# Forty unread products become fifty-four, and one gate-and-up product moves between two halves of a router's logits

## What is computed

```python
x = x + _L0_xattn_ref(_layernorm(x), ctx_2048)      # x, ctx to fp8 with scales, then one projection
x = x + _L0_ffn_ref(_layernorm(x), ...)             # 32 experts, 4 of them a token, one shared expert
x = x + _L1_xattn_ref(_layernorm(x), ctx_2048, ...) # 8 heads of softmax attention
x = x + _L1_ffn_ref(_layernorm(x), ...)             # 8 experts, 2 of them a token, shared expert
# _L0_ffn_ref:
logits = xf @ router_w.T + router_b
top_vals, top_idx = jax.lax.top_k(logits, K)
rw = softmax(top_vals) * SCALE
g, u = silu(x @ gate_w[e].T), x @ up_w[e].T
routed = sum over the chosen e of rw[e] * ((g * u) @ down_w[e].T)
shared = (silu(xf @ shared_gate_w.T) * (xf @ shared_up_w.T)) @ shared_down_w.T
```

## Time and profile before

| what | us |
|---|---|
| median of 3 runs | 417.14 (416.56 to 417.24) |
| the profiled execution | 417.1 |
| its span, first to last instruction | 415.3 |
| PE busy | 346.5 (83%) |
| DVE busy | 262.7 (63%) |
| ACT busy | 194.0 (47%) |
| POOL busy | 183.3 (44%) |

### The profile page before, as it was taken

The page is one execution under the profiler, slowest core; times in us unless marked ns, Lnnn a source line. Parts: engine busy times, 40 slices in busy tenths (PEclk is TensorE's granted clock), DMA queues, the critical chain, the costliest instruction groups (busy, mean ns, idle before and its releaser), DMA issues.

```text
span 415.3 us, 8257 instructions
## 1 busy us (share of the span) xinstructions
PE 346.5 (83%) x2383; PEld 195.8 (47%) x2383; DVE 262.7 (63%) x722; ACT 194.0 (47%) x453; POOL 183.3 (44%) x338
## 2 busy tenths in 40 slices
PE   0003298779999999999999978999987799998997
PEld 0002095444554555555454577666554354543455
DVE  2999848826555555555555488999877455555184
ACT  1341164344555555555554127999922445552110
POOL 2000300366766666676663107666610666753000
PEclk9999999999999999999999999999976999999899
DMA  7999993049222222323464387920011222331531
GB/s 227 396 255 333 319 266 106 1 139 281 88 97 88 93 90 89 103 85 95 113 186 158 125 333 215 255 59 2 2 47 56 85 82 88 100 95 39 175 106 51
DMA packets 28297, 57.32 MB, mean 138 GB/s; under 512 B 3806, under 2 KB 12734, under 8 KB 28254
## 3 DMA queue, kind: packets, MB, share of 16 engines
q1 hardware_dynamic: 20110, 37.85, 29.7%
q0 software_dynamic: 6528, 17.83, 14.1%
q10 hardware_dynamic: 1616, 1.11, 0.9%
HBM read 44.72 MB, written 12.06 MB: 137 GB/s over the span
## 4 chain that ended last, share of the span: by engine, by line
PE 69%; DVE 16%; issue 5%; ACT 4%; POOL 3%; DMA 2%; DVEq 0%; SPq 0%; ACTq 0%; POOLq 0%
PE bank L1308 22%; PE bank L1337 14%; PE bank L1319 6%; PE bank L1187 6%; PE bank L1299 4%; PE bank L1386 2%; PE bank L1398 2%; PE bank L1226 2%; PE bank L1200 2%; DMA x_sb<-x 2%; ACT arena L669 2%; DVE st L733 1%; DVE x_sb L1025 1%; PE bank L1154 1%; PE bank L1181 1%
## 5 line engine op out<-in xcount | busy, mean ns | idle before, releaser
L1308 PE MATMUL bank<-arena,xT 128*64 x272 | 111.2, 491 | 1.1 <-ACT xT L631 1.1
L1311 PE MATMUL bank<-xn,xT 128*64 128x384 f32 (+1 forms) x272 | 111.2, 491 | 0.0
L516 POOL DMA_INDIRECT xg<-m_xn,tab x68 | 66.2, 973 | 60.6 <-PE bank L1299 30.8
L505 POOL DMA_INDIRECT m_ys<-ysb,dest x68 | 67.2, 988 | 38.9 <-DVE ysb L945 22.4
L1337 PE MATMUL bank<-arena,hT 96*64 (+1 forms) x272 | 70.6, 381 | 2.4 <-DVE hT L931 2.3
L1340 PE MATMUL bank<-xn,hT 96*64 96x256 f32 (+1 forms) x272 | 70.7, 382 | 0.0
L624 ACT ACTIVATE xn<-arena 128x768 f32 (+1 forms) x68 | 56.3, 827 | 22.4 <-issue 22.4
L957 DVE TENSOR_TENSOR hh<-sg,bank 128x192 f32<-128x192 f32 (+1 forms) x71 | 24.8, 349 | 60.3 <-ACT sg L647 60.3
L1337 PEld LDWEIGHTS bank<-arena,hT 96*64 96x64 f32 (+1 forms) x272 | 34.7, 135 | 39.7 <-issue 29.3
L631 ACT ACTIVATE xT<-bank 128x256 f32<-128x256 f32 x71 | 27.2, 384 | 48.1 <-PE bank L1299 47.9
L925 DVE COPY xn<-arena 96x512 f32 (+1 forms) x68 | 29.2, 430 | 23.4 <-issue 23.4
(11 more groups left out here) (182 smaller groups left out, 564.9 us busy)
## 6 DMA issues: line engine op xcount, KB each, us to landing
arena<-w_gu SPq DMA_DIRECT2D x3, 3456.0 KB, 20.1
arena<-w_dn SPq DMA_DIRECT2D x3, 1728.0 KB, 26.5
arena<-m_ys SPq DMA_DIRECT2D x8, 512.0 KB, 6.5
arena<-w_gu SPq DMA_DIRECT2D x2, 1408.0 KB
m_xn<-xn SPq DMA_DIRECT2D x2, 1024.0 KB, 7.6
arena<-m_ys SPq DMA_DIRECT2D x8, 256.0 KB, 3.5
arena<-w_dn SPq DMA_DIRECT2D x2, 704.0 KB
arena<-w_gu SPq DMA_DIRECT2D x1, 1152.0 KB, 11.1
```

Of the source, the lines that this page charges most:

```text
L505: nc.gpsimd.indirect_dma_start(out=ys_d[L.name], out_offset=bass.IndirectOffsetOnAxis(ap=dest[:, s:s + 1], axis=0), in_=ysb[:, s % BUFS, : ...
L516: nc.gpsimd.indirect_dma_start(out=xg[:, b, :], out_offset=None, in_=xn_d[L.name], in_offset=bass.IndirectOffsetOnAxis(ap=d["tab"][:, s:s ...
L1308: T.matmul(bank[2 + s % 2][0:BLOCK, 0:2 * J2], xT[:, s % 2, c, 0:BLOCK], arena[:, bass.ds(off + c * 2 * J2, 2 * J2)], start=(c == 0), stop ...
L1311: return T.matmul(bank[2 + s % 2][BLOCK:P, 0:2 * J2], xT[:, s % 2, c, BLOCK:P], gu2[:, s % 2, cols], start=(c == 0), stop=(c == C - 1), ti ...
```

## The change

Three edits on PE's program. No other engine's program is changed.

```diff
+            def unread(n, b):
+
+                for _ in range(n):
+                    T.matmul(bank[b][:, 0:P], ident[:], ident[:], start=True, stop=True)
+
@@ routing
                 for i in range(NT // 2):
                     if L is L0 and i == 2:
+                        pe.wait_ge(*w_in)
+                        pe.wait_ge(x1_ready, NT)
+                        shared_steps(L, "early", 0, n_early[L.name], 0, 1)
                         turn_rows(L, 2)
                         turn_rows(L, 3)
@@
                 N = n_early[L.name]
                 pe.wait_ge(*w_in)
-                if L is L0:
-                    shared_steps(L, "early", 0, N, 0, 1)
-                else:
+                if L is L1:
                     pe.wait_ge(att_ready, NT)
@@
             pe.wait_ge(small_in, 64)
+            unread(14, 7)
             routing(L0, rw0, (w_shared, 32))
@@
-            def unread(n):
-
-                for _ in range(n):
-                    T.matmul(bank[5][:, 0:P], ident[:], ident[:], start=True, stop=True)
-
-            unread(26)
+            unread(26, 5)
             scores(0)
             scores(1)
             for p in range(nheads // 2):
                 turn_p(2 * p)
                 if p == 0:
-                    unread(14)
+                    unread(14, 5)
```

## The result

| kernel | median us | executions | ratio to before | 95% interval |
|---|---|---|---|---|
| before, in the same rounds | 418.76 | 16, 416.52 to 419.86 | | |
| changed | 415.47 | 16, 414.15 to 417.64 | 0.9932 | 0.9915 to 0.9949 |

The change is faster by 0.68% of 418.76, 2.85 us (2.1 to 3.6). The ratio is not that of the two medians: they differ by 3.29 us, the two means by 2.71. The three executions shown ahead of the prediction (417.14) were on the quick side of a kernel that scatters over 3 to 4 us, and the changed kernel's profiled execution (416.41 us, span 414.7) is on the slow side of its own. Set against the earlier trace rows, its trace shows the following.

What follows compares the result with a forecast made beforehand. PE at its slow clock was taken to bound the path through logits, mask and sums. Second-half logits 2.1 us earlier, 1.0 of late start included, less 0.1 for collision: 417.1 - 2.0 = 415.1 us, range 413.4 to 418.0.

Steps and rivals of the forecast that it cites:

- The path through logits and mask: Layer 0 routing: logits, mask and sums are one path on PE and DVE; all behind it, tiles included, starts 2.0 us earlier.
- Fourteen products raise the clock and it lasts: PE before the routing: the clock rises at 51.0 to 53.2 us, and both sets of sixteen logits take near 2.0.
- late start: First transposes on PE: products end at about 53.0 instead of 52.03, a cost of 1.0 us that nothing hides.
- The moved step: Between the logit halves: holds PE 1.3 us at the fast clock, now on the path; PE would have waited about 0.5.
- POOL beside DVE, 0.1: POOL's multiplication of the moved step falls beside DVE's second half; the collision costs the mask 0 to 0.5 us, taken as 0.1.
- The clock falls before step 1: PE is empty from 60.5 to about 64.1 us, so step 1 is expected slow again, as before.
- Rival B: Early shared steps: the clock rises one step later and step 2 pays 1.5 us, giving 416.6; chance 14%.
- The sum, 2.0: Whole kernel: second-half logits 2.1 us earlier, less 0.1 for the collision, carried through to the end.
- The time itself, 415.1: Whole kernel: profiled execution of 417.1 us less 2.0; likeliest case 414.5 to 415.7, at 54%.

Runs made afterwards that it cites:

- e9: The changed kernel run once more with nothing changed; 0.9937 of before, median 416.04 us.
- e5: The kernel before run once more with nothing changed, for a second profile; ratio 1.0005, median 418.95 us.
- e12: e11 with twelve instead of nine products in the wait for the mask and two in the wait for `cmp`; 0.9873 of before, 413.77 us.
- e8: The changed kernel with eight unread products in place of fourteen; 0.9976 of before, median 418.87 us.
- e1: The changed kernel without the move: fourteen products stay, step 0 goes back behind all logits; 0.9921 of before, 415.66 us.
- e10: The kernel of e1 (products only) run again beside the changed kernel; 0.9944 of before, median 416.07 us.
- e3: The changed kernel with fourteen more products between the last logits and the wait for the mask; 0.9937 of before, 416.29 us.
- e6: e1 with nine more products behind step 0, in the wait for the mask; 0.9927 of before, 415.21 us.
- e7: e6 with three further products behind each of the early steps 1 to 3; 0.9945 of before, 415.95 us.
- e11: e7 with five more products in the after step's wait and three in the first expert tile's wait; 0.9891 of before, 414.27 us.

## Why the prediction was right, and where it was off

**The path through logits and mask: right, and closer than its terms.** Measured from the last projection: first transposes 5.47 after it (predicted 5.7), second L829 13.24 (13.2), sums 16.95 (16.9). From the first transposes to the sums it is 11.48 where 11.2 was predicted; the clock rose early enough to make up for it here, and in e9, where the transposes start at the predicted 5.7, the sums are at 17.17. That one path runs from logits over mask to tiles is shown by e5 against the changed kernel, where the 2.04 of the sums arrive as 2.05 at the first tile.

**Fourteen products raise the clock and it lasts.** In all ten traces with fourteen products, or transposes for them, both sets of logits take 1.96 or 1.97. The rise came at 50.1 to 52.9, a little sooner than the 51.0 to 53.2 that I had from two rows, and at the earliest (e12) 2.3 us after the products began. So the late start was no fixed 1.0: it was 0.8 in the trace shown, and between nothing and 1.0 in the ten. At eight (e8) it did not last. That fourteen is enough in every execution isn't shown; the changed kernel's slowest (418.30 in e9) may be one where it was not, and its mean granted clock, 0.955, is near that of e8's trace (0.954).

**The moved step costs 1.3, of which PE would have waited 0.5: wrong in the second half.** The step holds PE 1.38, and without it the second logits start 1.34 earlier (e1, e10), so PE would have waited for nothing and the net cost is not 0.8. What I didn't see either is that DVE's first half would take over without it, so that only 0.6 of this reaches the sums, and nothing measurable the end. The move was part of the change and earned nothing; the gain is the products'.

**POOL beside DVE, 0.1: right for the wrong place.** The sums follow the second L829 by 3.71 in the changed kernel and 3.63 before. The collision is real but falls where the order puts it: the cast takes 0.39 longer in e1, and in e10 too.

**The clock falls before step 1: right** (2.77, as before). Rival B, step 2 slow, is what the profiled execution shows, so its trace alone would have said 0.2 us. Rival B was priced at 1.5 against a kernel before with a fast step 2; e5 shows that in the kernel before step 2 can take 2.77 too.

**The sum, 2.0, against 2.85 (2.1 to 3.6): low.** The term that was off is the carry from one execution to the median. I took the profiled execution as typical because three runs agreed with it. It is of the quick kind, with step 2 fast, and the changed kernel's is of the slow one. Like against like the gain is 2.3 to 2.8 in executions and 2.4 in the matched pair of traces, of which 0.4 is a chance collision. Where the other 0.3 to 0.8 arises isn't settled. A rarer slow kind is not the answer as far as the mean clocks show, 42 of 95 before and 14 of 28 after.

**The time itself, 415.1 against 415.47, is nearer than the argument deserves.** It is a base 1.6 too low (417.14 for 418.76) less a gain 1.3 too small by the medians (2.0 for 3.29), and the two errors partly cancel. As a ratio the forecast was 0.9952, just outside the measured 0.9915 to 0.9949.

## What to carry to other kernels

Where TensorE idles before a chain of small products, unread work in that idle time pays if it is long enough to raise the clock and its overrun is smaller than what the chain saves: here 5.1 us of it, which started the chain 0.8 us late (5.47 after the last projection, 4.72 before) and shortened it by 2.8. Here a clock held in one place fell in a later idle stretch (e3, e6, e7), and only filling nearly all waits up to the dense loop brought more (e11, e12), so count them first. And when single executions scatter by 3 us, compare traces only in pairs that show the same pattern of the clock, and look at the mean granted clock of every timed execution: it tells whether the trace is one of many or an exception.

## What the runs showed of the hardware

- The granted clock reads 1.00 until the trace's first change of it. In the kernel before, that is a rise at 74.1, ahead of which L1154's records take twice as long. Durations have to be read until then.
- 28 fp32 transposes raised the clock as 28 product records did (5.19 and 5.23 us).
- A DVE operation of 8 or 32 columns (L992, L839) took 0.17 to 0.18 us alone and 0.57 to 0.73 beside a GpSimd operation with two inputs of 192 or 256 columns. In the five traces looked at (before, e1, e5, e9, e10) it ended 0.03 us after the GpSimd operation. MAX8 and FIND_INDEX8 took no longer beside one (0.47 and 0.18).
- The mean granted clock of an execution goes with its time: 417.51 us at 0.974 or more and 419.39 at 0.971 or less, in 95 executions of the kernel before.
- With eight products the clock rose in the microsecond from 51 and fell in the one from 54, though PE had been idle for only 0.69 and 0.33 us between: transposes and narrow logits behind a short dense stretch did not keep it.
